# Alternating transposes and score products with a slot's job products on TensorE

## The reference

```
h = relu(layernorm(x))
q, k, v = heads(h @ Wq.T), heads(h @ Wk.T), heads(h @ Wv.T)
a = q @ k.T * 512 ** -0.5 + 2 * adj
p = softmax(a), 0 in rows where all of a is 0
out = x + (p @ v, heads joined) @ Wo.T
```

## Time and profile before

| | |
|---|---|
| median of 3 executions | 1319.92 us (1319.8 to 1320.41) |
| the profiled execution | 1319.87 us |
| its span, first to last instruction | 1318.1 us |
| TensorE busy (matmuls) | 1288.6 us, 98% |
| TensorE weight loads busy | 1225.6 us, 93% |
| VectorE busy | 1130.4 us, 86% |
| ScalarE busy | 1033.8 us, 78% |
| GpSimd busy | 902.1 us, 68% |
| mean granted clock of TensorE | 0.996 of full speed |

### The profile page before, as it was taken

How to read it: one execution, slowest core, us unless ns; L and a number is a source line. 1 busy time by engine, 2 the same in 40 slices (tenths; PEclk the granted TensorE clock), 3 DMA queues, 4 the chain that set the end, 5 groups by cost and what they waited for, 6 DMA issues and landing times. The chain is left out here.

```text
span 1318.1 us, 43774 instructions
## 1 busy us (share of the span) xinstructions
PE 1288.6 (98%) x13072; PEld 1225.6 (93%) x13072; DVE 1130.4 (86%) x4023; ACT 1033.8 (78%) x2379; POOL 902.1 (68%) x1263
## 2 busy tenths in 40 slices
PE   5899999999999999999999999999999999999996
PEld 5899999999999999999999999999999999999995
DVE  5888888888888888888889888888888888888884
ACT  3788778788787888887888787888788887788874
POOL 5667667667677676676776676776677776676765
PEclk9999999999999999999999999999999999999998
DMA  6445454455354454454454454454544554544441
GB/s 213 104 117 138 108 136 119 115 139 127 109 146 117 109 148 119 112 143 116 114 151 109 122 130 121 123 143 108 131 119 122 133 133 110 139 119 113 126 121 49
DMA packets 90772, 163.88 MB, mean 124 GB/s; under 512 B 14976, under 2 KB 23168, under 8 KB 90752
## 3 DMA queue, kind: packets, MB, share of 16 engines
q1 hardware_dynamic: 90752, 163.64, 47.9%
HBM read 46.14 MB, written 16.78 MB: 48 GB/s over the span
## 5 line engine op out<-in xcount | busy, mean ns | idle before, releaser
L849 POOL TENSOR_TENSOR fold<-minus 128x512 f32<-128x512 f32 x256 | 329.7, 1288 | 325.3 <-DVE bounds L703 325.3
L553 ACT ACTIVATE probs<-minus,bounds 128x256 f32<-128x256 f32 x1024 | 460.2, 500 | 19.1 <-DVE bounds L703 19.1
L564 ACT ACTIVATE pT_hi<-pT_ps 128x512 f16<-128x512 f32 x512 | 306.0, 598 | 154.3 <-PE pT_ps L401 152.6
L721 DVE TENSOR_TENSOR pT_lo<-pT_ps,pT_hi 128x512 f16<-128x512 f32 x512 | 351.1, 686 | 84.5 <-ACT pT_hi L564 84.2
L703 DVE CUSTOM_DVE_ANT_0 minus<-s_ps,adj_now 128x256 f32<-128x256 f32 x1024 | 389.3, 417 | 18.3 <-DVE adj_now L715 14.3
L401 PE MATMUL pT_ps<-ident,probs 128*128 128x128 f32 x2048 | 307.6, 273 | 1.7 <-ACT probs L553 1.6
L328 PE MATMUL job_ps<-hT_hi,w_hi 128*128 128x256 f32 x1024 | 300.4, 293 | 3.1 <-DVE hT_lo L671 2.6
L328 PE MATMUL job_ps<-hT_lo,w_hi 128*128 128x256 f32 x1024 | 290.1, 283 | 0.0
L328 PE MATMUL job_ps<-hT_hi,w_lo 128*128 128x256 f32 x1024 | 289.8, 283 | 0.0
L401 PEld LDWEIGHTS pT_ps<-ident,probs 128*128 128x128 f32 x2048 | 240.4, 140 | 15.4 <-ACT probs L553 2.6
L390 PE MATMUL s_ps<-qk_stack 96*128 96x256 f32 x1024 | 247.1, 323 | 2.2 <-DMA qk_stack<-qk_parts 2.2
(11 more groups left out here) (80 smaller groups left out, 2406.4 us busy)
## 6 DMA issues: line engine op xcount, KB each, us to landing
qk_stack<-qk_parts SPq DMA_DIRECT2D x768, 128.0 KB, 2.3
x_in<-x SPq DMA_DIRECT2D x32, 512.0 KB, 3.4
x_res<-x SPq DMA_DIRECT2D x32, 512.0 KB, 3.6
out<-y SPq DMA_DIRECT2D x64, 256.0 KB, 2.1
adj_in<-adj SPq DMA_DIRECT2D x32, 256.0 KB, 3.6
minus<-wq_t SPq DMA_DIRECT2D x2, 512.0 KB, 6.0
qk_parts<-wv SPq DMA_DIRECT2D x2, 512.0 KB, 10.5
y<-wk_t SPq DMA_DIRECT2D x1, 512.0 KB, 8.4
```

The costliest lines, as they stand in the source:

```text
L553: end = nc.scalar.activation(probs[hh % 2][:, t, :], minus[hh // 2 % 2][:, hh % 2, t, :], ACT.Exp, bias=bounds[:, hh // 2 % 4, 2 * (hh % 2 ...
L564: nc.scalar.activation(pT_hi[hh % 4][:, :, :], pT_ps[hh % 2][:, :].rearrange("p (m n) -> p m n", m=NT), ACT.Copy).then_inc(pT_high, 1)
L721: nc.vector.tensor_tensor(pT_lo[hh % 4][:, :, :], pT_ps[hh % 2][:, :].rearrange("p (m n) -> p m n", m=NT), pT_hi[hh % 4][:, :, :], ALU.sub ...
L849: nc.gpsimd.tensor_tensor(f1[:, :, :], src[:, :, 0:N // 2], src[:, :, N // 2:N], ALU.add).then_inc(folded1, 1)
```

## The change

TensorE no longer does the three groups of a slot one after another. After each of the 4 transposes and each of the 2 score products it does one instruction of the slot's jobs (`work`), then what is left of the jobs, and then, in even slots, the value products. To make this possible the jobs `h` and `o` are cut into 4 steps instead of 1. In slot 5, job h1 comes ahead of y0's second half instead of in its middle. h1 is now taken by ScalarE and VectorE at the end of slot 5 (`ended_in`) instead of in slot 6. The job qk0 waits for h0's low part when it begins and for that of h1 halfway through its first 12 products. The orders of ScalarE and VectorE are otherwise as they were, and so are the banks.

```
-PRODUCTS = {"qk": 24, "v": 12, "y": 12, "h": 1, "o": 1}
+PRODUCTS = {"qk": 24, "v": 12, "y": 12, "h": 4, "o": 4}
...
-    4: [("h", 0, 1, 0, 1), ("y", 0, -1, 0, 6)],
-    5: [("y", 0, -1, 6, 9), ("h", 1, 1, 0, 1), ("y", 0, -1, 9, 12)],
+    4: [("h", 0, 1, 0, 4), ("y", 0, -1, 0, 6)],
+    5: [("h", 1, 1, 0, 4), ("y", 0, -1, 6, 12)],
...
+TAKEN_AT_ONCE = ("h", 1)
...
+            def work(b, hh, first, last, start, stop):
+
+                at = 0
+                for kind, n, d, here, end in jobs_at(hh, first, last):
+                    lo, hi = max(here, here + start - at), min(end, here + stop - at)
+                    if lo < hi:
+                        job(kind, n, d, lo, hi, b)
+                    at += end - here
...
                 for hh in range(HEADS):
-                    transpose_probs(b, hh, first and hh < 2)
-                    if hh + AHEAD < HEADS:
-                        scores(b, hh + AHEAD)
-                    elif not last:
-                        scores(b + 1, hh + AHEAD - HEADS)
+                    done = 0
+                    for m in range(NT):
+                        for t in range(NT):
+                            transpose_probs(b, hh, m, t, first and hh < 2)
+                            work(b, hh, first, last, done, done + 1)
+                            done += 1
+                    for t in range(NT):
+                        if hh + AHEAD < HEADS:
+                            scores(b, hh + AHEAD, t)
+                        elif not last:
+                            scores(b + 1, hh + AHEAD - HEADS, t)
+                        work(b, hh, first, last, done, done + 1)
+                        done += 1
+                    work(b, hh, first, last, done, 1000)
 
                     for was in range(hh - 2, hh) if hh % 2 == 0 else ():
                         if was >= 0:
                             values(b, was, first and was < 2)
                         elif not first:
                             values(b - 1, HEADS + was, False)
-                    for kind, n, d, start, stop in jobs_at(hh, first, last):
-                        job(kind, n, d, start, stop, b)
...
                     high_probs(b, hh, first and hh < 4)
+                    for kind, n, d in ended_in(hh, first, last):
+                        take(kind, n, b + d)
...
                     low_probs(b, hh, first and hh < 2)
+                    for kind, n, d in ended_in(hh, first, last):
+                        take(kind, n, b + d)
```

More of the change, by code:

```diff
@@ L71, in ended_before, with ended_in @@
     if hh:
-        return [j[:3] for j in jobs_at(hh - 1, first, last) if j[4] == PRODUCTS[j[0]]]
+        return [j[:3] for j in jobs_at(hh - 1, first, last)
+                if j[4] == PRODUCTS[j[0]] and j[:2] != TAKEN_AT_ONCE]
     return [(kind, n, d - 1) for kind, n, d, _, end in JOBS[HEADS - 1]
             if end == PRODUCTS[kind] and not (first and d < 1)]
+def ended_in(hh, first, last):
+    return [j[:3] for j in jobs_at(hh, first, last) if j[:2] == TAKEN_AT_ONCE]
 def attention_block(nc, x, adj, wq_t, wk_t, wv, wo_t, out):
@@ L338, in job @@
                 if kind == "h":
-                    if n == 0:
+                    if n == 0 and start == 0:
                         pe.wait_ge(h_ready, b + (d + 1))
[L342 to L345, removed]
+                    for k, t in [divmod(i, NT) for i in range(start, stop)]:
+                        end = nc.tensor.transpose(ps[:, k * N + t * P:k * N + (t + 1) * P],
+                                                  h[:, t, (2 * n + k) * P:(2 * n + k + 1) * P], ident[:, :])
                 elif kind == "qk":
+                    half = PRODUCTS["qk"] // 2
                     if n == 0 and start == 0:
+                        pe.wait_ge(taken["h"], count("h", 0, b + d))
+                    if n == 0 and start <= half // 2 < stop:
                         pe.wait_ge(taken["h"], count("h", 1, b + d))
-                    half = PRODUCTS["qk"] // 2
                     for i, w in enumerate((WQ, WK)):
@@ L361, in job @@
                 elif kind == "o":
[L363 to L367, removed]
+                    if start == 0:
+                        pe.wait_ge(o_ready, (b + d) * PAIRS + 4 * (n + 1))
+                    for k, t in [divmod(i, NT) for i in range(start, stop)]:
+                        end = nc.tensor.transpose(ps[:, k * N + t * P:k * N + (t + 1) * P],
+                                                  o[:, t, (2 * n + k) * P:(2 * n + k + 1) * P], ident[:, :])
                 else:
@@ L379, in job @@
                     end.then_inc(ended[kind], 1)
[L381 to L387, removed]
-                stack = qk_stack[:, hh // HH, hh % G, :, hh % HH // G, :]
[L389 to L403, removed]
+            def work(b, hh, first, last, start, stop):
[5 more added lines that the diff above has]
+                    at += end - here
@@ new lines, in scores @@
+            def scores(b, hh, t, early=False):
+                if t == 0:
+                    if hh % HH < G:
+                        pe.wait_ge(stacked[hh % G], stack_count(hh // HH, b))
+                    if not early:
+                        pe.wait_ge(shifted, head_no(b, hh) + (1 - bank_before(hh)))
+                stack = qk_stack[:, hh // HH, hh % G, :, hh % HH // G, :]
+                end = nc.tensor.matmul(s_ps[SCORE_BANK[hh]][:, t * N:(t + 1) * N], stack[:, 0, t * P:(t + 1) * P],
+                                       stack[:, 1, :], start=True, stop=True)
+                if t == NT - 1:
+                    end.then_inc(scores_ready, 1)
@@ new lines, in transpose_probs @@
+            def transpose_probs(b, hh, m, t, early):
+                if m == t == 0:
+                    pe.wait_ge(exp_done, head_no(b, hh) + 1)
+                    if not early:
+                        pe.wait_ge(pT_split, head_no(b, hh) - 1)
+                end = nc.tensor.transpose(pT_ps[hh % 2][:, m * N + t * P:m * N + (t + 1) * P],
+                                          probs[hh % 2][:, t, m * P:(m + 1) * P], ident[:, :])
+                if m == t == NT - 1:
+                    end.then_inc(pT_ready, 1)
@@ L439, in _ @@
             for n in range(2):
-                job("h", n, 0, 0, 1, 0)
+                job("h", n, 0, 0, 4, 0)
             split_waits(pe, [(WQ, 1)])
@@ L454, in _ @@
             for hh in range(AHEAD):
-                scores(0, hh, True)
+                for t in range(NT):
+                    scores(0, hh, t, True)
             def body(b, first, last):
                 for hh in range(HEADS):
-                    transpose_probs(b, hh, first and hh < 2)
-                    if hh + AHEAD < HEADS:
-                        scores(b, hh + AHEAD)
-                    elif not last:
-                        scores(b + 1, hh + AHEAD - HEADS)
+                    done = 0
[4 more added lines that the diff above has]
+                            done += 1
+                    for t in range(NT):
+                        if hh + AHEAD < HEADS:
[5 more added lines that the diff above has]
+                    work(b, hh, first, last, done, 1000)
                     for was in range(hh - 2, hh) if hh % 2 == 0 else ():
@@ L482, in _ @@
                 values(B - 1, hh, False)
-            job("o", 1, -1, 0, 1, B)
+            job("o", 1, -1, 0, 4, B)
             for n in range(NT):
```

## The result

The median is 1561.74 us (1561.41 to 1562.63, four executions), against 1319.86 us for the kernel before beside it: 1.1834 times as long, with a 95% interval of 1.1814 to 1.1855. The profiled execution took 1562.63 us, its span is 1560.8 us, its mean granted clock 0.970 of full speed. The forecast was 1535 us, range 1440 to 1600.

A forecast was written before the change was run, and what follows sets the result against it. TensorE's own sequence was taken as the bound, 39.84 us a batch. 1320 us plus 193 us of net bank stalls plus 23 us of clock gave 1536, stated as 1535 us, range 1440 to 1600 us.

The forecast's parts named there:

- The alternation costs nothing: TensorE's transpose and product steps cost the same alternated as grouped, weight loads fitting under the running matmul: zero.
- 0.28 and 0.15 of gains: Per batch: 0.28 us from transposes following value products, 0.15 us from a swallowed wait for o1's low part.
- the upper bound of 0.4: Extra transpose-to-product steps in 16 slots, 0.008 us each if a product's load were 0.118 us: 0.4 us a batch.
- The opposite bound: If each of a batch's 80 transposes cost only its load, 0.07 for 0.11 us: 3.2 us a batch won.
- Value products last: Seven of eight value groups now followed by a transpose's shorter load, 0.04 us each: 0.28 us a batch gained.
- The stalls: TensorE waits for PSUM banks in slots 5, 6, 14, 3, 4 and 2: 6.6 us a batch in sum.
- 30 batches and the two ends: Net 6.2 us for each of 30 loop batches, 186 us; with first and last batch 193 us.
- The clock: Stalls of slots 4 to 6 lower TensorE's granted clock, 1.55 us a fall; half taken, 0.8 us a batch, 23 us.
- partly hidden: ScalarE and VectorE catch up, only slots 5 and 6 wait: about 1410 us; chance 0.09 with the slower several-loads-ahead form.
- Two falls of the clock a batch: Rival: TensorE's clock falls twice a batch, 6.2 + 3.1 us, 30 times, and 7 us: 1606 us, chance 0.09.
- The faster case: Rival: weight loads pulled further ahead, transposes cost 0.07 us; with only slot 5's wait 1285 us; chance 0.04.
- no change: Rival: banks come free unseen, some 0.4 us of waits balancing the gain; chance 0.02.

The follow-up runs named there:

- the third experiment: Kernel before with transposes and scores alternating with job products only in slots 0, 1, 7 to 13 and 15, values and h1 in old places: 1331.84 us, ratio 1.0101.
- the last experiment: Kernel before with order scores, values, transposes, jobs in slots 4, 6, 8, 10, 12, 14 of the loop's 30 batches only: 1310.3 us, ratio 0.9939.
- the first: Changed kernel with the value products put back directly behind the score products, alternation kept: 1464.93 us, ratio 1.1101.
- the fifth experiment: Changed kernel with ScalarE and VectorE taking h0 at the head of slot 5, ahead of copy, exponentials and shift: 1456.27 us, ratio 1.103.

## Why the prediction was right, by its steps

The mechanism and its places were right; the sum was 1.7% short. Of the 26 us that it lacked, 17 are the batch's (some 11 of the stalls, 6 of the alternation) and 10 the clock's, less 1 at the two ends.

- **The alternation costs nothing:** too low. A T P pair takes 0.23 us, as forecast, but unrounded it is some 0.006 us dearer than the steps apart (0.05 us for eight pairs). The batch gives what is left over: 6.76 us, less 6.97 of stalls, plus 0.28 and 0.15 of gains, is 0.22 us a batch, inside the upper bound of 0.4. The opposite bound, 3.2 us of gain, is refuted by the third experiment. That experiment also shows a price that no step from start to start holds: transposes that are spread out end later, which there cost more than the dearer pairs.
- **Value products last, 0.28 us:** not to be seen. Two slots without waits take 4.74 us before and after; what the shorter load gave, the pairs took. That it exists is shown by the last experiment, where it comes without the alternation.
- **The stalls:** 6.97 us for 6.6. Slot 5 2.55 for 2.50, slot 6 0.85 for 0.79, slot 14 0.74 for 0.72, slot 3 0.56 for 0.44, slot 4 1.22 for 1.15, slot 2 1.05 for 1.0 (each the gap to the job's first start, with the load that shows behind the wait, 0.05 to 0.11 us, less the steps due). The chain through the value products' new place is shown by the first and the fifth experiment.
- **30 batches and the two ends:** 30 x 6.76 = 203 us for 186. At the ends some 6 us for 7: that is what remains of 242 us after 203 and the 33 of the clock.
- **The clock:** 33 us for 23. Half a fall a batch was forecast, as a choice between none and one; 23 of 29 intervals had one, and without them the time is 33 us less, as the transposes put into the wait show. The size of one, 1.46 us, was near the 1.55 read from the earlier trace rows. The Trainium skill, "TensorE: Matmul & The Clock Gate", "A second HAM failure mode: psum-queue depth-cycling", says that small idle times between groups of matmuls, in a kernel that cycles through PSUM banks, make the clock swing. This trace agrees, with 1.46 us a swing, but a wait of some 1.35 us in slot 5 cost none (clock 0.997 in the first experiment).
- **The rivals:** partly hidden (1410 us) fell, since all six waits stayed in every batch. Two falls of the clock a batch (1606 us) fell: no interval is longer than 48.14 us. The faster case and no change fell with slot 5.

## What to carry to other kernels

Where TensorE is the bound and two buffers alternate, the work that stands between the release of a buffer and its next use is cover: an order that looks free on TensorE moves the start of the next job ahead, and the whole chain of the take becomes visible. Price a reordering by walking each buffer from the last product to the release through the strict queues of the other engines; that gave six stalls to within 0.12 us here. Spreading a group of instructions out also delays its end, and who waits for that end: in the third experiment this was 10 of 14 us. And count a long stall on TensorE as more than its length: it can also cost a fall of the clock, which transposes put into the wait avoided here.

## What was not expected of the hardware

- The batches without a fall came in a rhythm: among the 29 intervals they are the 1st, 3rd, 9th, 14th, 20th and 25th. All of these batches run the same instructions with the same waits; why the clock held in just these stays open.
- A program with 640 more transposes ran 33 us faster, by the clock alone.
- The first batch's clock hung on the order of its even slots: 0.90 from 40 to 88 us in one order, 1.00 in the other. In the order with 0.90 the clock is at 0.50 from 54 to 56 us, behind the wait of 1.67 us in front of h1, and from 74 to 76 us, behind that of 1.1 us in front of scores. It went back when the first and the last batch kept the old order; that these waits made it fall wasn't tried there.
